# The second layer norm of half 1 applied feature-major, with its moments spread by DMA

## The chip, the cores and the metric

One core of one Trainium2 chip runs the whole program. The metric is the device time of one execution in microseconds. Engines: PE (TensorE), DVE (VectorE), ACT (ScalarE), POOL (GpSimd) and SP (SyncE, which here only issues DMAs). Each works off its own list of instructions in order, and they meet at semaphores.

## The reference, cut to what matters

1024 tokens with 256 features. The first layer is a feed-forward whose weights for a token are one of four 256x256 context matrices, chosen by the token's id; the second is a mixture of 16 experts of width 96, four for each token, and a shared expert. Each layer gets the layer norm of x:

```
_layernorm(x) = (x - mean(x)) / sqrt(var(x) + 1e-5)        # over the 256 features
x = x + xattn(_layernorm(x), ids, ctx, ctx, ctx)
x = x + ffn(_layernorm(x), router, gate_up, down, shared)
  # ffn: scores = sigmoid(x @ router.T); top 4 by scores + bias, their scores divided by their sum
  #      routed = sum_e c_e * (silu(x @ gate_e.T) * (x @ up_e.T)) @ down_e.T, plus the shared expert
```

## The kernel before, in words

The tokens are two halves of 512 (h = 0, 1). All large products are feature-major: features on the partitions, tokens along the row, 512 wide. Every fp32 operand is split into a high part (rounded to fp32r) and a low part, and a product is three matmuls: high by low, high by high, low by high. The high part is made by ACT (or by DVE in the first layer), the low part by DVE (POOL for the weights).

The second layer is a list of 26 items (h, c), where c = 0 is the shared expert with the router's rows, and c = 1 to 12 are chunks of 128 of the 1536 routed features. Its order is (0,0) to (0,8), (1,0), (0,9) to (0,12), (1,1) to (1,12); g is an item's place in it, so place[1, 0] is 9 and place[1, 1] is 14. Pass g on PE (L1078 to L1093) is gate(g), up(g) (six matmuls each) and the down of item g - 2 (six, L1056 to L1059). Pass 11 has no down, and pass 16 has two, for item (1,0) and then for item 14. For each g, ACT makes silu of the gate (`silu_gate`, L528) and the high part of hid (`hid_high`, L538), and DVE the product with the router's weights (`product`, L800), hid (`hidden_2`, L813) and its low part (`hid_low`, L818). PE's gate(g) waits for silu(g - 2), up(g) for hid(g - 2), and down(g - 2) for both parts of hid.

The normalised x of half 1 is wanted at pass 9, and is made during the passes before:
- pass 2, PE: `x1_transposes` turn x1 (feature-major in xt) token-major into banks 5 and 4.
- pass 3, ACT: `copy_x1` moves them into x. DVE: `tile_stats`, `layer_norm_vars` of norm 3, from x. POOL: `rstd_of(3)`, the power -0.5 (L429).
- pass 5, DVE and ACT: `layer_norm_apply(3)`, `apply_norm(3)` write xn, token-major.
- pass 7, PE: `norm_transposes` (L917) turn xn back, eight transposes of 128x128 into banks 4 and 5, between up(7) and the down of item 5.
- pass 8, ACT: `x_high` (L463), DVE: `x_low` (L641), from those banks to xn_hi and xn_lo.

The router's rows of half 1 come out of gate(9). ACT copies them (`router_logits`, L519); DVE transposes them in lanes (`lane_logits`, L704), and over passes 10 to 12 finds the best four and the weights (`lane_best`, `lane_marks`, `lane_rows`). SP writes these to DRAM (`write_rows(1)`) and spreads them over partitions for item 14 on (`spread_rows`). At pass 15 DVE adds half 0's sums to xt (`output(0)`, L825), which frees the two sum banks for the down of item (1,0) at pass 16.

SP's list (L393 to L403) holds, after `write_rows(0)`, for each g the spread of item g (L390), the last two weight loads at g = 4 and 6 (L357), and the outputs. A spread's slot (two in x, two in ids) is free when the product four chunks back is done. POOL's list (L426 to L449) holds the powers and the low parts of the weights in the order of the pieces (`low_part`, L423, two instructions of 128x512 each), the power of norm 3 standing between pieces 10 and 11. ACT makes the high parts of pieces 12, 13 and 14 in passes 5, 6 and 7.

Of the kernel before, what the change touches and what calls it, by code (L numbers as in the profile page):

```python
# [28 lines left out]
P = 128  # L29
TOKENS = 1024  # L30
D = 256
# [19 lines left out]
WARM_UP = 20  # L51
LAG = 2
SENTINEL = -3.0e38
MARK = 3.0e38
# [24 lines left out]
def build(nc, x_d, xt_d, ids_d, ctx_d, bias_d, gu_d, wd0_d, wd_d, consts_d, out_d):  # L79
# [4 lines left out]
    with ExitStack() as ctx:  # L84
# [26 lines left out]
        power = sb("power", [P, TT])  # L111
        xn = sb("xn", [P, TT, D])
        xn_hi = sb("xn_hi", [P, HALVES, KC, HALF], F32R)
        xn_lo = sb("xn_lo", [P, HALVES, KC, HALF], F32R)
# [44 lines left out]
        rows_out, rows_copied = [sem(f"rows_out{h}") for h in range(HALVES)], sem("rows_copied")  # L159
        combt_zero, pick_rows_set, x1_copied = sem("combt_zero"), sem("pick_rows_set"), sem("x1_copied")  # L160
        dstep = sem("dstep")
        varied, powered, shifted = sem("varied"), sem("powered"), sem("shifted")
        normed_v, normed_a = sem("normed_v"), sem("normed_a")
        x1_turned = sem("x1_turned")
        side_done = sem("side_done")
        xhi_done, xlo_done = sem("xhi_done"), sem("xlo_done")
# [19 lines left out]
        for g in range(1, N):  # L186
            if g == 1:
                side_order += [("combt", 0, 0, 4)]
            if g <= BY_MATMUL:
                side_order += [("spread", *items[g], 4 + g % 2)]  # L190
            if g == BY_MATMUL:
                side_order += [("x1", 1, 0, 5), ("x1", 1, 1, 4)]
            if g == place[1, 0] - 2:
                side_order += [("n2", 1, 0, 4), ("n2", 1, 1, 5)]
        side_at = {u[:3]: n for n, u in enumerate(side_order)}

        def wait_side_read(eng, b, n):

            before = [u for u in side_order[:n] if u[3] == b]
            if not before:  # L200
                return
            what, h, k, _ = before[-1]
            if what in ("n1", "n2"):
                count = (HALVES * KC if what == "n2" else 0) + h * KC + k + 1
                eng.wait_ge(xhi_done, count)
                eng.wait_ge(xlo_done, count)
            elif what == "x1":
                eng.wait_ge(x1_copied, k + 1)
            elif what == "spread":
                eng.wait_ge(prod_done, routed(place[h, k]))  # L210
            elif what == "router":
                eng.wait_ge(logit_summed, h + 1)
            else:
                eng.wait_ge(rows_copied, h + 1)
# [119 lines left out]
        def tile_to_norm(n, t):  # L334

            if n != HALVES:
                return x[:, n % HALVES * TT + t]
            at = t % (TT // KC) * D
            return ring_bank("x1", 0, t // (TT // KC))[:, at:at + D]

# [9 lines left out]
        def _(sp):  # L350
# [32 lines left out]
            def spread_rows(g):  # L383
# [5 lines left out]
                for first, last, e in parts_of_chunk(c):  # L389
                    sp.dma_start(spread(n)[first:last],  # L390
                                 comb_d[h, e].partition_broadcast(last - first)).then_inc(spread_in[n % SPREADS], 16)

            write_rows(0)  # L393
            for g in range(BY_MATMUL + 1, N):
                if g == place[1, 1]:
                    write_rows(1)
                if items[g][1] > 0:
                    spread_rows(g)
                if g in (4, 6):
                    load_piece(len(pieces) - 2 + (g == 6))  # L400
                if g == place[1, SPREADS]:
                    write_output(0)
# [4 lines left out]
        def _(pool):  # L407
# [24 lines left out]
            nc.gpsimd.memset(biased_l[:, :, E2:], SENTINEL).then_inc(logits_zero, 1)  # L432
            nc.gpsimd.memset(comb_l[:], 0.0).then_inc(logits_zero, 1)
            nc.gpsimd.memset(combt[:].bitcast(F32), 0.0).then_inc(combt_zero, 1)
            rstd_of(0, 1, slice(0, TT // 2))
# [10 lines left out]
            low_part(early_pieces + 1)  # L446
            rstd_of(3, 5)
            for n in range(early_pieces + 2, len(pieces)):
                low_part(n)  # L449

        @block.scalar
        def _(act):
# [50 lines left out]

            def copy_x1(h):

                act.wait_ge(normed_v, HALVES * TT // 2)
                for pair in range(KC):
                    act.wait_ge(side_done, side_at["x1", h, pair] + 1)
                    at = h * TT + pair * (TT // KC)
                    nc.scalar.activation(x[:, at:at + TT // KC].rearrange("p t d -> p (t d)"),  # L510
                                         side_bank("x1", h, pair)[:], ACT.Copy).then_inc(x1_copied, 1)

# [64 lines left out]
            for g in range(1, N):  # L577
                if g == place[1, 0] - 1:
                    x_high("n2", 1, 0)
                    x_high("n2", 1, 1)  # L580
                if g == place[1, 0] + 1:
                    score(1)
                if g == place[1, 0]:
                    router_logits(1)
                if g == BY_MATMUL + 1:
                    copy_x1(1)
                silu_gate(g)
                if g == 1:
                    combine_rows(0)
                if g in late_pieces:  # L590
                    high_part(late_pieces[g])
                hid_high(g)
                if g == 5:
                    apply_norm(3)

        @block.vector
        def _(dve):
# [8 lines left out]
            def tile_stats(n, t):  # L606
                if n > HALVES:
                    dve.wait_ge(x1_copied, t // (TT // KC) + 1)
                elif n == HALVES:
                    dve.wait_ge(x1_turned, t // (TT // KC) + 1)  # L610
                step(nc.vector.bn_stats(stats[:, t], tile_to_norm(n, t)))  # L611
# [25 lines left out]
            def x_low(what, h, k):  # L637
                n = (HALVES * KC if what == "n2" else 0) + h * KC + k
                dve.wait_ge(xhi_done, n + 1)
                dve.wait_ge(side_done, side_at[what, h, k] + 1)  # L640
                nc.vector.tensor_tensor(xn_lo[:, h, k], side_bank(what, h, k)[:], xn_hi[:, h, k].bitcast(F32),  # L641
                                        ALU.subtract).then_inc(xlo_done, 1)

# [233 lines left out]
            for g in range(1, N):  # L877
                if g == place[1, 0] - 1:
                    x_low("n2", 1, 0)
                    x_low("n2", 1, 1)  # L880
                product(g)
                hidden_2(g)
                if g == place[1, 0]:
                    lane_logits()
# [9 lines left out]
                if g == 3:  # L894
                    for t in range(TT):
                        tile_stats(3, t)
                    layer_norm_vars(3)
                if g == 5:
                    layer_norm_apply(3)
            output(1)  # L900

        @block.tensor
        def _(pe):
# [18 lines left out]
            def x1_transposes(h, pair):  # L922
# [7 lines left out]
                for t in range(TT // KC):  # L930
                    at = h * HALF + (pair * (TT // KC) + t) * P
                    for k in range(KC):
                        ins = nc.tensor.transpose(b[:, t * D + k * P:t * D + (k + 1) * P], xt[:, k, at:at + P],  # L933
                                                  consts_sb[:, 0:P])
                ins.then_inc(x1_turned if h == 0 else side_done, 1)

            def mix(n, between={}):
# [140 lines left out]
            for g in range(1, N):  # L1078
# [4 lines left out]
                if g <= BY_MATMUL:  # L1083
                    spread_weights(g)
                if g == place[1, 0] - 2:
                    norm_transposes("n2", 3, 1)

                if g >= LAG and downs_at[g - LAG]:
                    for n in downs_at[g - LAG]:
                        down(n)  # L1090
                if g == BY_MATMUL:
                    x1_transposes(1, 0)
# [48 lines left out]
```

## Time and profile before

| what | us |
|---|---|
| median of three runs (lowest, highest) | 175.72 (175.63, 175.94) |
| the profiled execution | 175.69 |
| its span, first to last instruction | 173.6 |
| PE busy | 168.2 (97%) |
| DVE, ACT, POOL busy | 117.6, 68.1, 40.3 |

Times in views are from the start of the span. A matmul's row in the timeline overlaps the next one (0.40 long, one each 0.23); the chain of waits gives each the 0.23 that it holds the path for, and there a step stands some 0.16 later than its row in the timeline. An instruction's duration in the timeline counts from where it was issued on its engine, so that it holds time in which it was kept from its operands. The granted clock of PE is 0.999 over the span.

### The profile page before, as it was taken

To read this page: it belongs to the slowest core of one execution; us is meant where nothing else is said; L and a number is where in the kernel's file an instruction comes from. 1 tells how busy PE (TensorE), PEld (TensorE's weight loads), DVE (VectorE), ACT (ScalarE), POOL (GpSimd) and SP (SyncE) were. 2 spreads that over 40 slices of the span, in tenths; PEclk is the share of its full clock that TensorE was granted. 3 is DMA by queue.
4 is the path that set the end of the run, shared out by engine and by line. 5 is a ranking of instruction groups with operands and counts; after the bars stand their busy time and mean duration, and the time that the engine had idled before them with its cause. 6 is when DMAs were issued, how large, how long until landed. Compare 5 with 4: busy or idle time off the path is not lost.

```text
span 173.6 us, 2253 instructions
## 1 busy us (share of the span) xinstructions
PE 168.2 (97%) x738; PEld 131.9 (76%) x738; DVE 117.6 (68%) x267; ACT 68.1 (39%) x108; POOL 40.3 (23%) x41
## 2 busy tenths in 40 slices
PE   6989999999999999999999999999999999999992
PEld 2558888888888878888888788888878888878881
DVE  0779897885588697787688649995874544444452
ACT  2462431343115965724654582222332222222320
POOL 5593011674220006439385000000000000000000
PEclk9999999999999999999999999999999999999999
DMA  4999004065400006951111100004454221100003
GB/s 139 283 414 337 11 0 123 0 178 184 121 0 4 0 4 144 265 144 62 60 60 60 60 0 4 0 0 125 125 194 140 81 66 65 66 5 0 0 0 121
DMA packets 7451, 15.82 MB, mean 91 GB/s; under 512 B 1296, under 2 KB 1904, under 8 KB 7312
## 3 DMA queue, kind: packets, MB, share of 16 engines
q1 hardware_dynamic: 7440, 15.68, 28.5%
q8 instruction: 6, 0.10, 0.2%
q14 instruction: 5, 0.04, 0.1%
HBM read 14.56 MB, written 1.11 MB: 90 GB/s over the span
## 4 chain that ended last, share of the span: by engine, by line
PE 89%; DVE 3%; ACT 3%; DMA 2%; issue 1%; DVEq 0%; ACTq 0%
PE bank L955 24%; PE bank L1038 13%; PE bank L1037 13%; PE bank L1036 13%; PE bank L1056 7%; PE bank L1059 7%; PE bank L1057 7%; DMA x<-x_d 2%; PE bank L917 2%; PE bank L933 1%; DVE stats L611 1%; PE bank L1033 1%; PE bank L1032 1%; ACT L490 1%; ACT xn L480 1%
## 5 line engine op out<-in xcount | busy, mean ns | idle before, releaser
L1038 PE MATMUL bank<-xn_lo,gu_hi 128*128 128x512 f32 (+1 forms) x104 | 41.1, 395 | 0.0
L1036 PE MATMUL bank<-xn_hi,gu_lo 128*128 128x512 f32 x96 | 38.1, 397 | 0.0
L1037 PE MATMUL bank<-xn_hi,gu_hi 128*128 128x512 f32 x96 | 38.0, 395 | 0.0
L538 ACT ACTIVATE h_hi<-hid 128x512 fp32r<-128x512 f32 (+1 forms) x26 | 16.4, 632 | 44.4 <-DVE hid L813 44.4
L818 DVE TENSOR_TENSOR h_lo<-hid,h_hi 128x512 fp32r<-128x512 f32 (+1 forms) x26 | 21.6, 830 | 14.1 <-ACT h_hi L538 14.0
L1038 PEld LDWEIGHTS bank<-xn_lo,gu_hi 128*128 128x128 f32 (+1 forms) x104 | 19.4, 187 | 4.9
L528 ACT ACTIVATE act_sb<-bank 128x512 f32<-128x512 f32 (+1 forms) x26 | 15.4, 592 | 16.7 <-PE bank L1038 16.6
L423 POOL TENSOR_TENSOR gu_lo<-stage,gu_hi 128x512 fp32r<-128x512 f32 x12 | 16.8, 1417 | 21.4 <-ACT gu_hi L456 21.3
L1037 PEld LDWEIGHTS bank<-xn_hi,gu_hi 128*128 128x128 f32 x96 | 18.0, 188 | 4.3
L1036 PEld LDWEIGHTS bank<-xn_hi,gu_lo 128*128 128x128 f32 x96 | 18.0, 188 | 4.2
L662 DVE COPY_PREDICATED prod<-beyond,bank 128x512 f32<-128x512 uint8 x24 | 17.8, 740 | 4.9 <-PE bank L955 3.8
L1056 PE MATMUL bank<-h_hi,wd_lo 128*128 128x512 f32 (+1 forms) x52 | 20.8, 399 | 0.0
L1059 PE MATMUL bank<-h_lo,wd_hi 128*128 128x512 f32 (+1 forms) x52 | 20.6, 395 | 0.0
L1057 PE MATMUL bank<-h_hi,wd_hi 128*128 128x512 f32 (+1 forms) x52 | 20.6, 395 | 0.0
L813 DVE TENSOR_TENSOR hid<-prod,bank 128x512 f32<-128x512 f32 x24 | 16.5, 687 | 1.7
L800 DVE TENSOR_TENSOR prod<-act_sb,ids 128x512 f32<-128x512 f32 x10 | 7.6, 764 | 10.2 <-ACT act_sb L528 8.9
L800 DVE TENSOR_TENSOR prod<-act_sb,x 128x512 f32<-128x512 f32 x12 | 9.3, 778 | 7.1 <-ACT act_sb L528 7.1
L955 PE MATMUL bank<-xn_hi,ctx_hi 128*128 128x512 f32 x32 | 12.8, 400 | 0.7 <-ACT xn_hi L463 0.7
L955 PE MATMUL bank<-h_hi,ctx_hi 128*128 128x512 f32 x32 | 12.9, 403 | 0.0
L955 PE MATMUL bank<-xn_lo,ctx_hi 128*128 128x512 f32 x32 | 12.8, 399 | 0.0
L955 PE MATMUL bank<-xn_hi,ctx_lo 128*128 128x512 f32 x32 | 12.7, 396 | 0.0
L955 PE MATMUL bank<-h_lo,ctx_hi 128*128 128x512 f32 x32 | 12.7, 395 | 0.0
(104 smaller groups left out, 224.1 us busy)
## 6 DMA issues: line engine op xcount, KB each, us to landing
stage<-gu_d SPq DMA_DIRECT2D x6, 512.0 KB, 3.5
stage<-wd_d SPq DMA_DIRECT2D x3, 512.0 KB, 5.1
x<-comb_d SPq DMA_DIRECT2D x8, 192.0 KB, 2.8
ids<-comb_d SPq DMA_DIRECT2D x7, 192.0 KB, 2.7
stage<-ctx_d SPq DMA_DIRECT2D x4, 256.0 KB, 5.3
xt<-xt_d SPq DMA_DIRECT2D x1, 1024.0 KB, 9.5
x<-comb_d SPq DMA_DIRECT2D x8, 128.0 KB, 2.8
ids<-comb_d SPq DMA_DIRECT2D x6, 128.0 KB, 3.3
```

The source lines that it names most:

```text
L423: ins = nc.gpsimd.tensor_tensor(lo[:, s], st[:, s], hi[:, s].bitcast(F32), ALU.subtract)
L662: nc.vector.copy_predicated(prod[:, n % 2], beyond[:, e - 1, h * HALF:(h + 1) * HALF], ring_bank("z", n, e)[:]).then_inc(z_picked, 1)
L800: nc.vector.tensor_tensor(prod[:, g % 2], act_sb[:, g % 2], rows, ALU.mult).then_inc(prod_done, 1)
L813: nc.vector.tensor_tensor(hid[0:w, g % 2], src, up_bank(g)[0:w, :], ALU.mult).then_inc(hid_done, 1)
L818: nc.vector.tensor_tensor(h_lo[0:w, slot[g]], hid[0:w, g % 2], h_hi[0:w, slot[g]].bitcast(F32), ALU.subtract).then_inc(hlo_done, 1)
L955: return nc.tensor.matmul(ring_bank("z", n, e)[:], (ctx_hi, ctx_lo)[a][:, e, k, f], parts[k][b], start=start, stop=stop)
L1036: nc.tensor.matmul(out[:], gu_lo[:, cols], xn_hi[:, h, k], start=(k == 0), stop=False)
L1037: nc.tensor.matmul(out[:], gu_hi[:, cols], xn_hi[:, h, k], start=False, stop=False)
L1038: ins = nc.tensor.matmul(out[0:rows, :], gu_hi[:, wide], xn_lo[:, h, k], start=False, stop=(k == KC - 1))
L1056: nc.tensor.matmul(acc[k][:], wd_lo[0:w, c, cols], hi, start=(c == 0), stop=False)
L1057: nc.tensor.matmul(acc[k][:], wd_hi[0:w, c, cols], hi, start=False, stop=False)
L1059: ins = nc.tensor.matmul(acc[k][:], wd_hi[0:w, c, cols], lo, start=False, stop=(c == ITEMS - 1))
```

## The change

- PE: the eight transposes L917 of pass 7 are gone. In their place, behind down(2) in pass 4, one 128x128 transpose turns a tile `moments` whose columns 0 to 3 are the means of the four token tiles and columns 4 to 7 the rstds, so that rows 0 to 7 of bank 4 are mean and rstd of all 512 tokens.
- DVE: statistics of norm 3 read x1's banks themselves; the means are copied to `moments`; `layer_norm_apply(3)` is gone. In pass 7, between hid and its low part, two multiplications by the rstd row (`x1_scale`); in pass 8 `x1_low` in place of `x_low`, from SBUF.
- ACT: `copy_x1` and `apply_norm(3)` are gone; `copy_moments` (8x128) stands in pass 4 ahead of `hid_high(4)`; `x1_high` in place of `x_high`, from SBUF.
- POOL: one more memset (128x128); the power writes into `moments`; behind low_part(12) two subtractions of the mean row from xt, 128x512 each, ahead of low_part(13).
- SP: behind the spread of item 5, the write of 8x128 to DRAM, a wait for it, and its broadcast to all partitions (512 KB, into xn); all later spreads and the last weight load stand behind.

```diff
+MOMENTS_AT = 4
+CENTRE_BEHIND = 12
+        moments = sb("moments", [P, P])
+        moments_t = sb("moments_t", [2 * TT, P])
+        moments_d = nc.dram_tensor("moments_d", (2 * TT, P), F32, kind="Internal").ap()
+        moments_all = xn[:].rearrange("p t d -> p (t d)")
+        mean_all, rstd_all = moments_all[:, 0:HALF], moments_all[:, HALF:]
+        x1_norm = x[:, TT:].rearrange("p t d -> p (t d)")
...
+            def write_moments():
+                sp.wait_ge(moments_copied, 1)
+                sp.dma_start(moments_d, moments_t[:]).then_inc(moments_out, 16)
+                sp.wait_ge(moments_out, 16)
+                sp.dma_start(moments_all, moments_d.rearrange("r c -> (r c)").partition_broadcast(P)).then_inc(moments_in, 16)
+                if g == MOMENTS_AT + 1:
+                    write_moments()
...
+            nc.gpsimd.memset(moments[:], 0.0).then_inc(moments_zero, 1)
-            rstd_of(3, 5)
+            pool.wait_ge(varied, NORMS + 1)
+            pool.wait_ge(moments_zero, 1)
+            nc.gpsimd.tensor_tensor(moments[:, TT:2 * TT], vareps[:, 3], power[:], ALU.pow).then_inc(powered, 1)
             for n in range(early_pieces + 2, len(pieces)):
                 low_part(n)
+                if n == CENTRE_BEHIND:
+                    for k in range(KC):
+                        pool.wait_ge(moments_in, 16)
+                        nc.gpsimd.tensor_tensor(x1_norm[:, k * HALF:(k + 1) * HALF], xt[:, k, HALF:], mean_all,
+                                                ALU.subtract).then_inc(centred, 1)
...
-            def copy_x1(h):
+            def copy_moments():
+                act.wait_ge(side_done, side_at["moments", 1, 0] + 1)
+                nc.scalar.activation(moments_t[:], side_bank("moments", 1, 0)[0:2 * TT, 0:P], ACT.Copy).then_inc(moments_copied, 1)
+            def x1_high(k):
+                act.wait_ge(x1_normed, k + 1)
+                act.wait_ge(z_done, (mixed[1, 1, KC - 1] + 1) * E1)
+                nc.scalar.activation(xn_hi[:, 1, k], x1_norm[:, k * HALF:(k + 1) * HALF], ACT.Copy).then_inc(xhi_done, 1)
                 if g == place[1, 0] - 1:
-                    x_high("n2", 1, 0)
-                    x_high("n2", 1, 1)
+                    x1_high(0)
+                    x1_high(1)
-                if g == BY_MATMUL + 1:
-                    copy_x1(1)
                 silu_gate(g)
...
+                if g == MOMENTS_AT:
+                    copy_moments()
                 hid_high(g)
-                if g == 5:
-                    apply_norm(3)
...
+            def x1_scale():
+                dve.wait_ge(moments_in, 16)
+                for k in range(KC):
+                    dve.wait_ge(centred, k + 1)
+                    o = x1_norm[:, k * HALF:(k + 1) * HALF]
+                    nc.vector.tensor_tensor(o, o, rstd_all, ALU.mult).then_inc(x1_normed, 1)
+            def x1_low(k):
+                dve.wait_ge(xhi_done, (HALVES + 1) * KC + k + 1)
+                dve.wait_ge(x1_normed, k + 1)
+                nc.vector.tensor_tensor(xn_lo[:, 1, k], x1_norm[:, k * HALF:(k + 1) * HALF], xn_hi[:, 1, k].bitcast(F32),
                                         ALU.subtract).then_inc(xlo_done, 1)
             for g in range(1, N):
                 if g == place[1, 0] - 1:
-                    x_low("n2", 1, 0)
-                    x_low("n2", 1, 1)
+                    x1_low(0)
+                    x1_low(1)
                 product(g)
                 hidden_2(g)
+                if g == place[1, 0] - 2:
+                    x1_scale()
...
                     layer_norm_vars(3)
-                if g == 5:
-                    layer_norm_apply(3)
+                    dve.wait_ge(moments_zero, 1)
+                    nc.vector.tensor_copy(moments[:, 0:TT], meanvar[:, 3, :, 0]).then_inc(means_set, 1)
...
+            def moments_transpose():
+                pe.wait_ge(means_set, 1)
+                pe.wait_ge(powered, NORMS + 1)
+                b = side_wait("moments", 1, 0)
+                nc.tensor.transpose(b[:, 0:P], moments[:], consts_sb[:, 0:P]).then_inc(side_done, 1)
...
-                if g == place[1, 0] - 2:
-                    norm_transposes("n2", 3, 1)
                 if g >= LAG and downs_at[g - LAG]:
                     for n in downs_at[g - LAG]:
                         down(n)
+                if g == MOMENTS_AT:
+                    moments_transpose()
```

## Rows read from the trace of the kernel before

**Rows 1.** The page: busy time by engine, and the chain's share by engine.

```profile
PE 168.2 (97%) x738; PEld 131.9 (76%) x738; DVE 117.6 (68%) x267; ACT 68.1 (39%) x108; POOL 40.3 (23%) x41
...
PE 89%; DVE 3%; ACT 3%; DMA 2%; issue 1%; DVEq 0%; ACTq 0%
```

**Rows 2.** The chain in order of time, passes 5 to 9: start, length, what.

```profile
78.20 0.23 PE bank L1036
...
86.60 0.23 PE bank L1036
...
89.40 0.87 PE bank L917 x8
...
91.66 0.23 PE bank L1036
...
95.86 0.23 PE bank L1032
```

**Rows 3.** The same, pass 16: the first matmul of item (1,0)'s down.

```profile
126.65 0.50 PE bank L1056
```

**Rows 4.** Who waited for whom: us in total, times, longest.

```profile
PEld bank L1056 <- DVE xt L825: 0.4, 1, 0.4
```

**Rows 5.** Timeline of DVE: start, length, line, what, idle before.

```profile
99.45 0.71 DVE L704 STREAM_TRANSPOSE comb_row<-logits 32x512 f32<-32x512 f32 x1
...
121.27 0.69 DVE L800 TENSOR_TENSOR prod<-act_sb,ids 128x512 f32<-128x512 f32 x1 [1.31 <-DMA ids<-comb_d]
```

**Rows 6.** Timeline of POOL and DVE about the powers of norms 2 and 3.

```profile
50.25 1.01 POOL L429 TENSOR_TENSOR rstd<-vareps,power 128x4 f32<-128x4 f32 x1 [5.66 <-DVE vareps L620]
...
76.62 0.69 DVE L800 TENSOR_TENSOR prod<-act_sb,x 128x512 f32<-128x512 f32 x1
...
76.79 1.39 POOL L429 TENSOR_TENSOR rstd<-vareps,power 128x4 f32<-128x4 f32 x1 [5.30 <-DVE vareps L620]
```

**Rows 7.** Timeline of all engines about the combine transposes.

```profile
61.71 0.40 PE L1038 MATMUL bank<-xn_lo,gu_hi 128*128 128x512 f32 x1
...
61.98 0.22 DVE L782 TENSOR_TENSOR comb_parts<-comb_parts 128x64 fp32r<-128x64 f32 x1
...
62.64 0.47 PE L1036 MATMUL bank<-xn_hi,gu_lo 128*128 128x512 f32 x1
```

**Rows 8.** Timeline of ACT, passes 4 and 9.

```profile
78.06 0.64 ACT L538 ACTIVATE h_hi<-hid 128x512 fp32r<-128x512 f32 x1 [2.03 <-DVE hid L813]
...
97.34 0.59 ACT L519 ACTIVATE logits<-bank 32x512 f32<-32x512 f32 x1 [0.28 <-PE bank L1038]
```

**Rows 9.** DMA issues, whole span, then 71 to 78: KB each, us to landing.

```profile
stage<-gu_d SPq DMA_DIRECT2D x6, 512.0 KB, 3.5
...
comb_d<-comb_row SPq DMA_DIRECT2D x2, 32.0 KB, 1.6
...
stage<-gu_d SPq DMA_DIRECT2D x1, 512.0 KB, 5.8
```

**Rows 10.** Timeline of POOL, passes 5 to 7, in narrow windows.

```profile
82.81 1.29 POOL L423 TENSOR_TENSOR gu_lo<-stage,gu_hi 128x512 fp32r<-128x512 f32 x1
...
87.37 2.99 POOL L423 TENSOR_TENSOR wd_lo<-stage,wd_hi 128x512 fp32r<-128x512 f32 x2 [3.26 <-ACT wd_hi L456]
...
88.62 1.74 POOL L423 TENSOR_TENSOR wd_lo<-stage,wd_hi 128x512 fp32r<-128x512 f32 x1
```

**Rows 11.** Timeline of DVE, passes 7 and 8.

```profile
88.48 0.73 DVE L818 TENSOR_TENSOR h_lo<-hid,h_hi 128x512 fp32r<-128x512 f32 x1 [0.70 <-ACT h_hi L538]
89.14 1.77 DVE L800 TENSOR_TENSOR prod<-act_sb,x 128x512 f32<-128x512 f32 x1
90.94 0.69 DVE L813 TENSOR_TENSOR hid<-prod,bank 128x512 f32<-128x512 f32 x1
...
93.80 1.27 DVE L641 TENSOR_TENSOR xn_lo<-bank,xn_hi 128x512 fp32r<-128x512 f32 x2
...
95.71 0.69 DVE L813 TENSOR_TENSOR hid<-prod,bank 128x512 f32<-128x512 f32 x1
```

More of the change, by code:

```diff
@@ L159, in build @@
         rows_out, rows_copied = [sem(f"rows_out{h}") for h in range(HALVES)], sem("rows_copied")
-        combt_zero, pick_rows_set, x1_copied = sem("combt_zero"), sem("pick_rows_set"), sem("x1_copied")
+        combt_zero, pick_rows_set = sem("combt_zero"), sem("pick_rows_set")
         dstep = sem("dstep")
@@ L164, in build @@
         x1_turned = sem("x1_turned")
+        moments_zero, means_set, moments_copied = sem("moments_zero"), sem("means_set"), sem("moments_copied")
+        moments_out, moments_in = sem("moments_out"), sem("moments_in")
+        centred, x1_normed = sem("centred"), sem("x1_normed")
         side_done = sem("side_done")
@@ L192, in build @@
                 side_order += [("x1", 1, 0, 5), ("x1", 1, 1, 4)]
-            if g == place[1, 0] - 2:
-                side_order += [("n2", 1, 0, 4), ("n2", 1, 1, 5)]
+            if g == MOMENTS_AT:
+                side_order += [("moments", 1, 0, 4)]
         side_at = {u[:3]: n for n, u in enumerate(side_order)}
@@ L207, in wait_side_read @@
             elif what == "x1":
-                eng.wait_ge(x1_copied, k + 1)
+                eng.wait_ge(varied, NORMS + 1)
+            elif what == "moments":
+                eng.wait_ge(moments_copied, 1)
             elif what == "spread":
@@ L334, in tile_to_norm @@
         def tile_to_norm(n, t):
[L336 to L339, printed above, removed]
+            at, pair = t % (TT // KC) * D, t // (TT // KC)
+            if n < HALVES:
+                return x[:, n * TT + t]
+            if n == HALVES:
+                return ring_bank("x1", 0, pair)[:, at:at + D]
+            return side_bank("x1", 1, pair)[:, at:at + D]
         def wait_normed(eng, n, t):
@@ L502, in combine_rows @@
                 nc.scalar.activation(comb_row[2 * E2:3 * E2, h], side_bank("combt", h, 0)[2 * E2:3 * E2, :], ACT.Copy).then_inc(rows_copied, 1)
-            def copy_x1(h):
[L506 to L511, printed above, removed]
+            def copy_moments():
[5 more added lines that the diff above has]
+                nc.scalar.activation(xn_hi[:, 1, k], x1_norm[:, k * HALF:(k + 1) * HALF], ACT.Copy).then_inc(xhi_done, 1)
             def router_logits(h):
@@ L607, in tile_stats @@
                 if n > HALVES:
-                    dve.wait_ge(x1_copied, t // (TT // KC) + 1)
+                    dve.wait_ge(side_done, side_at["x1", 1, t // (TT // KC)] + 1)
                 elif n == HALVES:
@@ L641, in x_low @@
                 nc.vector.tensor_tensor(xn_lo[:, h, k], side_bank(what, h, k)[:], xn_hi[:, h, k].bitcast(F32),
+                                        ALU.subtract).then_inc(xlo_done, 1)
+            def x1_scale():
[8 more added lines that the diff above has]
+                nc.vector.tensor_tensor(xn_lo[:, 1, k], x1_norm[:, k * HALF:(k + 1) * HALF], xn_hi[:, 1, k].bitcast(F32),
                                         ALU.subtract).then_inc(xlo_done, 1)
@@ L1084, in _ @@
                     spread_weights(g)
-                if g == place[1, 0] - 2:
-                    norm_transposes("n2", 3, 1)
                 if g >= LAG and downs_at[g - LAG]:
@@ L1090, in _ @@
                         down(n)
+                if g == MOMENTS_AT:
+                    moments_transpose()
                 if g == BY_MATMUL:
```

## Prediction, made before the result was known

> **What bounds the kernel now.** I read the busy shares and the shares of the chain first: PE is busy 97% of the span and has 89% of the chain [rows 1]. Then the chain in order of time: the passes of the second layer (g = 1 to 25, one per item) stand on a fixed grid. A pass is 12 matmuls of gate and up and 6 of down, 4.20 us (91.66 to 95.86); pass 7 holds the eight L917 transposes besides and takes 5.06 (86.60 to 91.66), so they cost **0.86 us of PE's path**, not hidden by anything [rows 2]. Last, the waits and the late part of the chain: PE waits once for another engine in this stretch, at 126.65, for DVE's output of half 0 before the down of item (1,0): that step is 0.50 instead of 0.23, so 0.27 lost [rows 3, 4]. That output stands at the end of a chain of DVE and ACT work that begins at pass 9 (router logits, lane transpose at 99.45, best four, rows to DRAM, spread back with a DMA wait at 121.27) [rows 5]. So two things end together: PE's grid, and this router chain, which is already 0.27 late.
>
> **Part 1, the transposes go.** -0.86 us on PE at pass 7, if nothing else is late [rows 2].
>
> **Part 2, the moments' transpose at pass 4.** PE comes to it after down(2), at 78.20 on the chain, its weight load being wanted one matmul and some (0.39) earlier, at 77.81. It waits for the power on POOL. The statistics now read PSUM instead of x, and the ACT copies go; but DVE is held before them by h_lo(3), so their place stays. Before, POOL's power starts at 76.79 and ends at 78.18; it takes 1.39 against 1.01 at 50.25, as prod (L800, two SBUF inputs) ran from 76.62 to 77.31 [rows 6]. The new copy of the means (four columns) shifts that product by 0.08, so the power ends at 78.26: 0.45 late. What such lateness costs is seen at the combine transposes: their input lands at 62.20 (61.98 + 0.22), 0.49 after the load of L1038's successor was due (61.71), and the next gate matmul comes 0.93 after L1038, where four transposes at 0.11 and one step of 0.23 make 0.67: 0.26 to 0.3 lost [rows 7]. So 0.28 for the wait and 0.11 for the transpose itself (0.86/8): **+0.39**. Bounds: 0.11 if the power gets in ahead of the product (then it ends at 77.8), 0.8 if it is held by a whole further op. Passes 5 to 7 run 0.39 late, pass 8 on 0.47 early; pass 9 would start at 95.39.
>
> **Part 3, ACT and SP at pass 4.** copy_moments stands ahead of hid_high(4), which ran at 78.06 [rows 8]; the copy can start near 78.75 and takes about 0.3 (an estimate: ACT's smallest rows are 0.26 to 0.6), so hid_high(4) ends at 79.6. down(4) wants it at pass 6: hidden. SP then writes the 4 KB (1.6 to land, as comb_d) and issues the 512 KB broadcast at 80.65. It lands in 3.5 us as the free weight loads do, or 5.8 as the load at 71.56 that shared the queue with spreads: 84.2 to 86.4 [rows 9]. I take 84.8, as the queue is empty when it is issued. Behind the two waits on SP stand the spreads of items 6, 7 and 8 and the last weight load, about 1.3 MB, which before were under way by then; at the pace of [rows 9] they land from 85 to 89.5, about when DVE and ACT want them. The new memset on POOL ends before POOL's first power and costs nothing.
>
> **Part 4, POOL and DVE, the deciding part.** x_low read a PSUM bank (L641, two in 1.27) [rows 11]. Now there are two subtractions on POOL of the form of its low parts, 1.29 each when free, and on DVE two multiplications and two x1_low whose inputs both lie in SBUF. The rows show that such a DVE op and a POOL op exclude each other: prod at 89.14 took 1.77 instead of 0.69, ending 0.55 after POOL's pair that began at 87.37 (so its own 0.69 began 0.14 before POOL's end); and POOL's second op took 1.74 instead of 1.29 as h_lo held it at 88.48. hid at 90.94, with a PSUM input, ran its 0.69 under a busy POOL. And they alternate: h_lo and prod stood back to back on DVE, and POOL got in between them [rows 10, 11].
>
> The Trainium skill, SBUF — State Buffer, "Who interferes with whom", says that a DVE instruction with two SBUF inputs contends with a GpSimd instruction that reads SBUF, one with at most one SBUF input does not, and whoever issues first holds the shared pair for the whole instruction; the trace agrees (1.77 against 0.69). It does not say who is next when both want it; if DVE kept it over two ops in a row, the sum would be that of rival A.
>
> Queued behind the new waits are, on POOL, low_part(13) and (14) behind centre, and on DVE h_lo(7) and pass 8 behind the two scales. By 0.69, 1.29 and 0.14 at each handover, in us: POOL ends low_part(12) at 84.4 (82.81 + 1.29 and 0.26 for the later silu and h_lo(4)) [rows 10]; centre(0) 84.8 to 86.1; prod(6) is held to 86.0-86.6; centre(1) 86.5-87.8; hid(6) 86.7-87.4, ACT's h_hi(6) to 88.0; low_part(13) has POOL 87.8-89.1 and 89.5-90.8 with h_lo(6) between them (to 89.6); prod(7) 90.6-91.3; hid(7) to 92.0; low_part(14) first half 91.2-92.5; scale(0) 92.3-93.0; second half 92.9-94.2; scale(1) 94.05-94.7. DVE then is free of POOL: h_lo(7) to 95.4, x1_low(0) to 96.0, x1_low(1) to 96.7, prod(8), hid(8) to **98.07**. Before, hid(8) ended at 96.40 (95.71 + 0.69) [rows 11]. With the broadcast at 85.0 and prod(6) first, the order differs but h_lo(7) waits for the last POOL op and hid(8) again ends at 98.07.
>
> **Part 5, what this does.** PE at pass 9 wants x1_low(0) at 95.39 + 0.47 - 0.39 = 95.47 and has it at 96.0: some 0.45 lost. That alone would make the change worth nothing (-0.86 + 0.39 + 0.45). But ACT does h_hi(8) after hid(8), then the router's logits, then silu(9), and DVE hid(9) and the lane transpose. In order these take 0.03 + 0.6 + 0.6 + 0.6 + 0.03 + 0.72 = 2.58, so the lane transpose starts at 98.07 + 2.58 = 100.65 instead of 99.45: **1.2 us later**; before it was PE's gate(9) that set it (logits at 97.34 waited 0.28 for PE) [rows 5, 8]. From there to the output at pass 15 every piece is DVE, ACT or DMA in a row, with no POOL work left and no slack (the chain ends 0.27 after PE asks). So PE, wherever it stands meanwhile (on the old grid within 0.1), waits about 1.4 at down of item (1,0), and all that follows is 1.2 later than before.
>
> **Sum.** The profiled execution took 175.69, of which 173.6 is the span; the median of the three runs is 175.72, 0.03 more. Span 173.6 + 1.2 = 174.8, time 175.72 + 1.2 = **176.9**.
>
> **Rivals.**
> A, faster: DVE keeps the port over ops back to back, or is never held long. Then h_lo(6), prod(7) end by 90.3, the two scales by 92.7, x1_low(1) by 94.6, hid(8) by 96.0. That is before the point that decides, hid(8) at 96.4: there PE's gate(9) sets the logits, and the whole chain moves with PE. 175.72 - 0.86 + 0.39 = 175.25. For it: POOL's spans are rough, and one pair of rows is all there is on who comes next. Against it: the alternation at 89.14 [rows 10, 11].
> B, much slower: the broadcast or the spreads land late, 5.8 us instead of 4.1 [rows 9]. centre(0) runs 86.4-87.7, each later POOL op falls between two DVE ops, x1_low(0) itself is held to 96.8, and hid(8) ends at 98.84: 96.87 is the value at which the lane chain is unmoved, so +1.97, 177.7. For it: 1.3 MB queue up behind the moments.
> C, no change: the router chain has slack that I don't see, and only the waits of pass 4 and pass 9 count: -0.86 + 0.39 + 0.45 = 0, 175.7. Against it: PE's wait at 126.65 [rows 3, 4].
>
> **Chances.** Forecast 0.52, A 0.16, B 0.20, C 0.12. 0.2% (0.35 us) is about what a measurement of this kernel tells from no change. A is faster; C is mostly the same (0.09), else slower (0.03); with the forecast and B that is 0.75 slower. The range is 175.4 to 178.0: it takes in B, C and the bound of 0.8 of part 2, and leaves out the middle of A and a pile-up worse than B. The forecast's own range is 176.2 to 177.3, hid(8) at 97.4 to 98.5.
>
> **What would show it.** L917 has 24 transposes instead of 32, and pass 7 is 4.2 us. Pass 4 to 5 shows 0.4 us more on PE, with the power named as releaser. The multiplications by rstd, or h_lo(7) and prod(7), last over 1.2 us while POOL works. hid of item 8 ends near 98; the lane transpose (L704's line) starts near 100.6; PE's step at down of item (1,0) is near 1.6 instead of 0.50. If hid(8) ends before 96.4 and that step is still 0.5, A is right; if the lane transpose is late but PE's step at pass 16 is not long, C is.

## The result, and the profile after

The changed kernel takes 177.38 us (median of 6) against 175.75: ratio 1.0089, interval 1.007 to 1.0107, **slower by 1.6 us**. The forecast was 176.9 in 175.4 to 178.0. One of the six, the profiled one, ran at a granted clock of 0.66 and took 239.26 us; the ratio is without it, and the median of the other five is 177.15. The profile shown is therefore that of a repeat run of the same kernel, `after_same`: median 176.99, ratio 1.0083, profiled execution 177.43, the longest of its four.

The page's heads, which answer to [rows 1]: PE's share falls from 97% to 95%, and of the chain that ended last from 89% to 61%; DVE and DMA now have 25% of it.

```profile
span 175.6 us, 2241 instructions
...
PE 167.3 (95%) x731; PEld 130.7 (74%) x731; DVE 118.3 (67%) x267; ACT 66.8 (38%) x105; POOL 42.5 (24%) x44
...
PE 61%; DVE 15%; DMA 10%; ACT 6%; issue 5%; SPq 1%; DVEq 0%; ACTq 0%
```

PE's timeline, in the three places where it now stands still (start, length, line): pass 4, pass 9, and the down of item (1,0) at pass 16.

```profile
77.37 0.40 PE L1114 MATMUL bank<-h_lo,wd_hi 128*128 128x512 f32 x1
77.92 0.30 PE L990 MATMUL bank<-consts_sb,moments 128*128 128x128 f32 x1 [0.16 <-issue]
78.05 0.47 PE L1091 MATMUL bank<-xn_hi,gu_lo 128*128 128x512 f32 x1
78.36 0.39 PE L1092 MATMUL bank<-xn_hi,gu_hi 128*128 128x512 f32 x1
...
95.15 0.40 PE L1088 MATMUL bank<-xn_hi,gu_lo 128*96 128x512 f32 x1
96.44 0.50 PE L1093 MATMUL bank<-xn_lo,gu_hi 128*128 128x512 f32 x1 [0.89 <-DVE xn_lo L687]
96.77 0.39 PE L1087 MATMUL bank<-xn_hi,gu_hi 128*128 128x512 f32 x1
...
126.62 0.40 PE L1093 MATMUL bank<-xn_lo,gu_hi 128*128 128x512 f32 x1
128.31 0.50 PE L1111 MATMUL bank<-h_hi,wd_lo 96*128 96x512 f32 x1 [1.29 <-DVE xt L871]
```

The step at pass 16 in PE's timeline of the kernel before, which answers to [rows 3]:

```profile
126.24 0.40 PE L1038 MATMUL bank<-xn_lo,gu_hi 128*128 128x512 f32 x1
126.65 0.50 PE L1056 MATMUL bank<-h_hi,wd_lo 96*128 96x512 f32 x1
```

A matmul follows the last by 0.23 where nothing holds it. So pass 4 costs 0.45 more (77.37 to 78.05 is 0.68, less 0.23), pass 9 1.06 more (1.29 less 0.23), and the step at pass 16 is 1.69 from start to start, where it was 0.41 before: 1.28 more. The matmul behind each new wait also starts late, after 0.31 and 0.33 instead of 0.23. With -0.86 for the transposes these make 0.45 + 0.08 + 1.06 + 0.10 + 1.28 - 0.86 = +2.11.

Executions differ ahead of the second layer and behind the last matmul: here the front is 0.45 shorter after the change and the tail 0.33 longer. So I compare profiles by T, the time from the start of PE's first x1 transpose of half 1 (68.78 before, 68.33 after) to the start of its last matmul (169.91, 171.58): 101.13 before, **103.25** after, +2.12, which these terms account for.

What DVE and POOL do in passes 6 to 9, the answer to [rows 11] and [rows 10]:

```profile
87.01 1.64 DVE L846 TENSOR_TENSOR prod<-act_sb,ids 128x512 f32<-128x512 f32 x1 [2.56 <-DMA ids<-comb_d]
88.69 0.69 DVE L859 TENSOR_TENSOR hid<-prod,bank 128x512 f32<-128x512 f32 x1
90.08 0.69 DVE L864 TENSOR_TENSOR h_lo<-hid,h_hi 128x512 fp32r<-128x512 f32 x1 [0.70 <-ACT h_hi L571]
91.08 0.69 DVE L846 TENSOR_TENSOR prod<-act_sb,x 128x512 f32<-128x512 f32 x1 [0.31 <-DMA x<-comb_d]
91.80 0.69 DVE L859 TENSOR_TENSOR hid<-prod,bank 128x512 f32<-128x512 f32 x1
92.41 2.77 DVE L681 TENSOR_TENSOR x<-x,xn 128x512 f32<-128x512 f32 x2
95.10 0.68 DVE L864 TENSOR_TENSOR h_lo<-hid,h_hi 128x512 fp32r<-128x512 f32 x1
95.70 1.28 DVE L687 TENSOR_TENSOR xn_lo<-x,xn_hi 128x512 fp32r<-128x512 f32 x2
96.90 0.68 DVE L846 TENSOR_TENSOR prod<-act_sb,x 128x512 f32<-128x512 f32 x1
97.62 0.69 DVE L859 TENSOR_TENSOR hid<-prod,bank 128x512 f32<-128x512 f32 x1
...
100.96 0.71 DVE L750 STREAM_TRANSPOSE comb_row<-logits 32x512 f32<-32x512 f32 x1
```

```profile
84.16 2.71 POOL L479 TENSOR_TENSOR x<-xt,xn 128x512 f32<-128x512 f32 x2 [0.26 <-DMA xn<-moments_d]
86.82 2.99 POOL L446 TENSOR_TENSOR wd_lo<-stage,wd_hi 128x512 fp32r<-128x512 f32 x2
91.56 3.07 POOL L446 TENSOR_TENSOR gu_lo<-stage,gu_hi 128x512 fp32r<-128x512 f32 x2 [1.75 <-ACT gu_hi L487]
```

hid of item 8 ends at 98.31 (96.40 before), the two scales take 2.77 under POOL's low parts, and the lane transpose starts at 100.96 (99.45 before [rows 5]). But there is a wait that the forecast had as hidden: prod(6) stands 2.56 us for its spread. The DMA view of 76 to 90 us (busy tenths of the DMA engines in 40 slices of 0.35 us; then issues, KB each, median us to landing) shows why. The spread of item 6 is issued behind the broadcast and ahead of the last weight load, the spreads of items 7 and 8 behind both, and the engines are nearly full from 81 to 89.

```profile
DMA  0000000000000069999599884999999999999745
...
ids<-comb_d SPq DMA_DIRECT2D x3, 192.0 KB, 6.1
xn<-moments_d SPq DMA_DIRECT2D x1, 512.0 KB, 4.3
stage<-gu_d SPq DMA_DIRECT2D x1, 512.0 KB, 8.3
...
x<-comb_d SPq DMA_DIRECT2D x1, 192.0 KB, 6.1
x<-comb_d SPq DMA_DIRECT2D x1, 64.0 KB, 8.7
```

### The profile page after: what moved, and what is told of

The parts are those of the page before. It is cut to its first block, busy times and chain, and to the rows that moved or that the text cites. A ratio compares the mean times of both kernels' runs of the same rounds, so it can differ in the third digit from the quotient of the medians.

```text
span 237.4 us, 2241 instructions
## 1 busy us (share of the span) xinstructions
PE 231.9 (98%) x731; PEld 146.2 (62%) x731; DVE 115.6 (49%) x267; ACT 68.2 (29%) x105; POOL 41.0 (17%) x44
## 4 chain that ended last, share of the span: by engine, by line
PE 98%; ACT 0%; POOL 0%; DVE 0%; issue 0%; DVEq 0%; POOLq 0%
PE bank L1010 26%; PE bank L1093 14%; PE bank L1091 13%; PE bank L1092 13%; PE bank L1112 7%; PE bank L1111 7%; PE bank L1114 7%; PE bank L1123 3%; PE bank L965 2%; PE bank L1088 1%; PE bank L981 1%; PE bank L1087 1%; PE bank L1038 0%; PE bank L1045 0%; ACT xn_hi L494 0%; PE bank L1055 0%
## 5 line engine op out<-in xcount | busy, mean ns | idle before, releaser
L1093 PE MATMUL bank<-xn_lo,gu_hi 128*128 128x512 f32 (+1 forms) x104 | 52.9, 509 | 0.0
L1091 PE MATMUL bank<-xn_hi,gu_lo 128*128 128x512 f32 x96 | 49.1, 512 | 0.0
L1092 PE MATMUL bank<-xn_hi,gu_hi 128*128 128x512 f32 x96 | 48.7, 507 | 0.0
L1112 PE MATMUL bank<-h_hi,wd_hi 128*128 128x512 f32 (+1 forms) x52 | 26.5, 510 | 0.0
L1111 PE MATMUL bank<-h_hi,wd_lo 128*128 128x512 f32 (+1 forms) x52 | 26.3, 507 | 0.0
L1114 PE MATMUL bank<-h_lo,wd_hi 128*128 128x512 f32 (+1 forms) x52 | 26.2, 504 | 0.0
L1010 PE MATMUL bank<-xn_hi,ctx_hi 128*128 128x512 f32 x32 | 16.4, 511 | 0.6 <-ACT xn_hi L494 0.6
L1010 PE MATMUL bank<-h_hi,ctx_hi 128*128 128x512 f32 x32 | 16.5, 516 | 0.0
L1010 PE MATMUL bank<-xn_lo,ctx_hi 128*128 128x512 f32 x32 | 16.3, 508 | 0.0
L1010 PE MATMUL bank<-h_lo,ctx_hi 128*128 128x512 f32 x32 | 16.3, 508 | 0.0
```

What stands on the lines that cost most here:

```text
L1010: return nc.tensor.matmul(ring_bank("z", n, e)[:], (ctx_hi, ctx_lo)[a][:, e, k, f], parts[k][b], start=start, stop=stop)
L1091: nc.tensor.matmul(out[:], gu_lo[:, cols], xn_hi[:, h, k], start=(k == 0), stop=False)
L1092: nc.tensor.matmul(out[:], gu_hi[:, cols], xn_hi[:, h, k], start=False, stop=False)
L1093: ins = nc.tensor.matmul(out[0:rows, :], gu_hi[:, wide], xn_lo[:, h, k], start=False, stop=(k == KC - 1))
L1111: nc.tensor.matmul(acc[k][:], wd_lo[0:w, c, cols], hi, start=(c == 0), stop=False)
L1112: nc.tensor.matmul(acc[k][:], wd_hi[0:w, c, cols], hi, start=False, stop=False)
```

## Experiments

The question after the result: is the loss the port between POOL and DVE (the forecast), the spreads that come late behind the moments (rival B), or PE's own waits (rival C); and is the router chain really without slack? Times stand against runs of the kernel before on the same chip.

**1. after_same**: the changed kernel unchanged.

> The changed kernel as it is, for a profile at full clock. My theory (the recorded forecast, with the measured 1.009): span 175.2 to 175.8. hid of item 8 ends at 98.0 to 98.7, the lane transpose starts near 100.6 to 101.2, and PE's step at the down of item (1,0), pass 16, is 1.6 to 2.1 us instead of 0.50. Rival (only PE's own waits at passes 4, 9 and between): the time is lost on PE before pass 10, and the step at pass 16 stays near 0.5.

Measured: as shown above. The long step at pass 16 is there (1.69), and so is a loss at pass 9 (1.06) that was larger than forecast. The rival, loss before pass 10 alone, is out.

**2. hold_pool**: POOL's last low parts wait.

```diff
             for n in range(early_pieces + 2, len(pieces)):
+                if n == CENTRE_BEHIND + 1:
+                    pool.wait_ge(xlo_done, NORMS * KC)
                 low_part(n)
```

> The changed kernel with POOL's low parts of the last two weight pieces held until both x1_low are done, so that they no longer meet the scales and x1_low on DVE. Port theory: the scales and h_lo(7) run in 0.69 each, hid of item 8 ends by 96.5, PE loses nothing at pass 9, the whole is 0.8 to 1.6 us faster than the changed kernel (175.6 to 176.5; the low parts now meet product(8) and h_lo(8) instead). Rival (the moments arrive late by DMA, the port is not it): within 0.3 of the changed kernel, 177.2.

Measured: 175.97, ratio 1.0019 (1.0004 to 1.0035), 1.1 us better than the changed kernel. The scales run at 0.69 each and PE loses nothing at pass 9:

```profile
87.16 0.69 DVE L848 TENSOR_TENSOR prod<-act_sb,ids 128x512 f32<-128x512 f32 x1 [2.54 <-DMA ids<-comb_d]
...
92.14 1.28 DVE L683 TENSOR_TENSOR x<-x,xn 128x512 f32<-128x512 f32 x2
93.34 0.69 DVE L866 TENSOR_TENSOR h_lo<-hid,h_hi 128x512 fp32r<-128x512 f32 x1
...
95.87 0.69 DVE L861 TENSOR_TENSOR hid<-prod,bank 128x512 f32<-128x512 f32 x1
97.26 1.53 DVE L866 TENSOR_TENSOR h_lo<-hid,h_hi 128x512 fp32r<-128x512 f32 x1 [0.70 <-ACT h_hi L573]
...
100.16 1.32 DVE L755 TENSOR_TENSOR laned<-comb_row 32x256 f32<-32x256 f32 x1
```

The port is the larger cause: 1.1 us is won with the low parts only moved. The late spread stays (2.54), and the held low parts now meet h_lo(8) and laned (1.32 instead of 0.42), on the router chain: the step at pass 16 is still 1.48.

**3. low_memset**: the two last low parts as memsets.

```diff
+                if n > CENTRE_BEHIND:
+                    pool.wait_ge(w_hi, n + 1)
+                    for part in range(2):
+                        s = slice(part * STAGE // 2, (part + 1) * STAGE // 2)
+                        ins = nc.gpsimd.memset(piece_aps(n)[3][:, s].bitcast(F32), 0.0)
+                    ins.then_inc(w_lo, 1)
+                    continue
                 low_part(n)
```

> Leaves out work: the low parts of the last two weight pieces are set to zero by POOL memsets, which read nothing from SBUF, instead of being computed. Port theory: nothing is left on POOL that reads SBUF after the two subtractions of the mean; hid of item 8 ends at 95.5 to 96.3, the lane transpose starts at or before 99.4, and the time is 175.2 to 175.6 (before less 0.86 plus 0.4). Rival (late moments or spreads): 177.0 to 177.4, as the changed kernel.

Measured: 175.52, ratio 0.9996 (0.9973 to 1.0019): 1.5 us better than the changed kernel, as the port theory has it. The single executions lie from 175.2 to 176.8, and the profiled one was the slowest: there the moments' write took 2.35 us instead of 1.19, prod(6) stood 3.96 for its spread, hid(8) ended at 97.87 and the lane transpose started at 100.52. So the expected hid(8) and lane transpose were missed in that profile while the median met the time. With no low part left to meet DVE, what is late there comes by DMA: that path is a cause of its own, and a varying one.

**4. late_lanes**: before, with 1.3 us of DVE work ahead of the lane transpose.

```diff
                 if g == place[1, 0]:
+                    for part in range(KC):
+                        src = ctx_hi[:, part].rearrange("p k f -> p (k f)").bitcast(F32)
+                        dve.wait_ge(w_hi, E1)
+                        dve.wait_ge(w_lo, E1)
+                        dve.wait_ge(z_done, len(mixes) * E1)
+                        nc.vector.tensor_tensor(ctx_lo[:, part].rearrange("p k f -> p (k f)"), src, src, ALU.add)
                     lane_logits()
```

> The kernel before, with two DVE additions of 128x512 whose result nobody reads put ahead of the lane transpose in pass 9 (1.3 us). If the router chain has no slack, as I hold, PE's step at pass 16 grows from 0.50 to 1.8 and the time from 175.7 to 177.0. If it has slack (rival C), the time stays at 175.7 to 175.9.

Measured: 176.14, ratio 1.002 (1.0001 to 1.0039), neither: 0.35 of the 1.3 comes through in the ratio, 0.58 in T of the one profile. The timelines of DVE and ACT show slack at one place in the chain, first in the kernel before, then in this run:

```profile
100.19 0.42 DVE L707 TENSOR_TENSOR laned<-comb_row 32x256 f32<-32x256 f32 x1
...
100.10 1.28 ACT L490 ACT_TABLE_LOAD   x1
```

```profile
100.97 0.42 DVE L707 TENSOR_TENSOR laned<-comb_row 32x256 f32<-32x256 f32 x1
...
99.04 0.64 ACT L538 ACTIVATE h_hi<-hid 96x512 fp32r<-96x512 f32 x1 [0.89 <-DVE hid L813]
99.69 1.28 ACT L490 ACT_TABLE_LOAD   x1
101.42 0.41 ACT L493 ACTIVATE scores_l<-laned 32x256 f32<-32x256 f32 x1 [0.45 <-DVE laned L707]
```

The sigmoid needs laned and the table load; before, laned is ready at 100.61 and the load is through at 101.38, so that laned has 0.8 of slack. Here laned is ready at 101.39 and the load through at 100.97, and the sigmoid waits 0.45 for laned. So in the kernel before the chain does not run over the lane transpose but over silu(9), hid(9), h_hi(9) and the table load on ACT.

**5. late_act**: before, with 1.15 us of ACT work in that path.

```diff
                     router_logits(1)
+                    act.wait_ge(w_lo, E1)
+                    act.wait_ge(z_done, len(mixes) * E1)
+                    for part in range(KC):
+                        nc.scalar.activation(ctx_lo[:, part], ctx_hi[:, part].bitcast(F32), ACT.Copy)
```

> The kernel before, with two ACT copies of 128x512 whose result nobody reads put between the router's logits and silu(9) in pass 9 (1.2 us). late_lanes showed 0.8 us of slack between laned and the sigmoid, as the load of the sigmoid table behind h_hi(9) was later than laned. If the chain runs through ACT (silu(9), hid(9), h_hi(9), table load) and has no slack there, product(10) starts 1.1 to 1.2 later and PE's step at pass 16 grows from 0.4 to 1.5, time 176.8 to 177.0. If the chain has slack there too, the time stays under 176.2.

Measured: 176.88, ratio 1.0061 (1.0039 to 1.0083): +1.07 for 1.15 put in, 0.7 to 1.5 by the interval. PE's step at pass 16 is 1.68 (0.41 before). With that, what the forecast needed of the chain is shown: ACT's lateness in pass 9 is PE's at pass 16, about one to one.

**6. spreads_first**: the changed kernel, moments behind the spreads on SP.

```diff
-                if g == MOMENTS_AT + 1:
+                if g == MOMENTS_AT + 4:
                     write_moments()
```

> The changed kernel with the moments' write and broadcast issued on SP behind the spreads of items 6, 7 and 8 and the last weight load, which then no longer wait for the moments (in the changed kernel prod(6) and prod(7) waited 2.56 and 0.31 for those spreads). DMA theory (the late spreads are the cause of about 1 us of the loss, the port of the rest): hid of item 8 ends 0.7 to 1.7 us earlier than 98.3, PE's loss at pass 9 falls from 1.06 to 0.5 or less, and the time is 175.8 to 176.6. Rival (the port alone sets it, as my working before had it): hid of item 8 still ends at 98.0 or later, 176.9 to 177.2.

Measured: 177.25, ratio 1.0081 (1.0059 to 1.0104): no gain (T of the one profile is 102.81, 0.44 below the changed kernel). The time is the rival's: no product of passes 6 to 8 waits for a spread any more, and now the port takes all of it. The edit is not a clean removal of the DMA's part, though. The moments are now the ones that come late: the broadcast is issued at 81.43 instead of 79.76, and POOL's subtractions start at 85.70 instead of 84.16, having waited 1.41 for it, which puts its low parts later too.

```profile
87.17 1.63 DVE L864 TENSOR_TENSOR h_lo<-hid,h_hi 128x512 fp32r<-128x512 f32 x1 [0.70 <-ACT h_hi L571]
89.16 1.35 DVE L846 TENSOR_TENSOR prod<-act_sb,x 128x512 f32<-128x512 f32 x1 [0.36 <-ACT act_sb L561]
...
91.14 2.77 DVE L681 TENSOR_TENSOR x<-x,xn 128x512 f32<-128x512 f32 x2
93.84 1.78 DVE L864 TENSOR_TENSOR h_lo<-hid,h_hi 128x512 fp32r<-128x512 f32 x1
...
97.46 0.69 DVE L859 TENSOR_TENSOR hid<-prod,bank 128x512 f32<-128x512 f32 x1
```

This is the forecast's own order of events: h_lo(6), prod(7), the scales and h_lo(7) each held by a POOL instruction. hid(8) ends at 98.15, where the forecast had 98.07, and the front is that of before (first x1 transpose at 68.74 against 68.78). PE's loss at pass 9 is 0.49 (a step of 0.72, less 0.23), where the forecast had 0.45, and the step at pass 16 is 1.81.

**7. spreads_hold**: edits 2 and 6 together.

> The same, and POOL's low parts of the last two pieces held until both x1_low are done. If late spreads and the port together explain the loss, hid of item 8 ends by 95.8 and the time is 175.3 to 175.9, at or below the kernel before. If something else makes the chain late (the moments' own path over DRAM), it is no better than hold_pool, 176.0.

Measured: 175.69, ratio 0.9996 (0.998 to 1.0012). hid(8) ends at 94.73 and T is 100.90. Both causes gone, the change costs nothing, and gains nothing yet.

**8. moments_ready**: PE turns other data in pass 4, which leaves out the right moments.

```diff
-                pe.wait_ge(means_set, 1)
-                pe.wait_ge(powered, NORMS + 1)
                 b = side_wait("moments", 1, 0)
-                nc.tensor.transpose(b[:, 0:P], moments[:], consts_sb[:, 0:P]).then_inc(side_done, 1)
+                nc.tensor.transpose(b[:, 0:P], xt[:, 0, HALF:HALF + P], consts_sb[:, 0:P]).then_inc(side_done, 1)
```

> The changed kernel, whose PE turns 128 columns of xt instead of the moments in pass 4, so that it waits for nothing there (leaves out the right moments: the norm of half 1 is wrong). The wait of PE (0.45 with the transpose itself) shrinks to 0.11. My theory: PE's grid is not what ends last at pass 16, so the gain is not 0.34; what counts is that the moments leave for DRAM 0.35 earlier, and with them the spreads: the time falls by 0.2 to 0.4, to 176.6 to 177.0, with the step at pass 16 as long as before or longer. Rival (PE's grid counts): the step at pass 16 stays the same and everything is 0.34 earlier. If the spreads' lateness comes from the amount of data and not from when it starts: no change at all, 177.1.

Measured: 176.64, ratio 1.0058 (1.0038 to 1.0078), some 0.4 better than the changed kernel by the ratios (1.0083 and 1.0089), though the intervals overlap. That is what my theory and the first rival both give, and the step at pass 16, 1.45, came out shorter than either had. prod(6) waits 0.73 for its spread instead of 2.56. But `after_out` (experiment 12), which is the changed kernel with PE's wait left in and differs from it only from pass 15 on, has the same in its profile: prod(6) waits 0.88 and hid(8) ends at 97.57, here at 97.55.

```profile
85.53 0.83 DVE L846 TENSOR_TENSOR prod<-act_sb,ids 128x512 f32<-128x512 f32 x1 [0.88 <-DMA ids<-comb_d]
...
96.88 0.69 DVE L859 TENSOR_TENSOR hid<-prod,bank 128x512 f32<-128x512 f32 x1
```

So the spread's wait in the changed kernel varies from execution to execution, and this experiment does not decide what sets it.

**9. moments_mid**: spreads_hold, with the moments turned where PE need not wait.

```diff
                 gate_or_up(g, False)
+                if g == MOMENTS_AT + 1:
+                    moments_transpose()
...
-                if g == MOMENTS_AT:
-                    moments_transpose()
...
+                hid_high(g)
                 if g == MOMENTS_AT:
                     copy_moments()
-                hid_high(g)
```

> spreads_hold, with the moments' transpose between gate(5) and up(5), 1.4 us later, so that PE doesn't wait for the power, and the copy behind h_hi(4) on ACT. PE's 0.45 at pass 4 becomes 0.11, gate(9) and with it the router chain come 0.34 earlier; the moments land about 1.1 later, which the scales (DVE gets to them near 90) don't feel. My theory: 0.3 us faster than spreads_hold, 175.3 to 175.5, ratio 0.997 to 0.9985. Rival: the router chain takes its own time from its DMAs on and nothing is gained, 175.7.

Measured: 175.07, ratio 0.9953 (0.9937 to 0.997), faster than before by 0.8 us, and by the ratios 0.8 below spreads_hold (taken on another chip), where 0.3 was expected. T is 100.77, 0.36 below before and 0.13 below spreads_hold (100.90); where the rest of the 0.8 comes from, the profile of one execution does not show. The step at pass 16 is 0.77 here and 0.54 in spreads_hold: the router chain ends last again.

**10. moments_mid_out**, **11. before_out**, **12. after_out**: output(0) ahead of product(15), on moments_mid, on before and on the changed kernel.

```diff
+                if g == place[1, 1] + 1:
+                    output(0)
                 product(g)
                 hidden_2(g)
...
-                if g == place[1, 1] + 1:
-                    output(0)
                 hid_low(g)
```

> moments_mid, with output(0) on DVE ahead of product(15) instead of behind hid(15), so that the router chain ends 1.3 us earlier as PE sees it. If that chain was what ended last at pass 16, PE's step there falls to 0.23 and the time to 175.0 to 175.3, ratio 0.9955 to 0.998. If hid(15), now later, holds up(17), no gain against moments_mid.

> The kernel before with output(0) ahead of product(15). PE's step at pass 16, 0.50 with 0.18 to 0.27 of wait, becomes 0.23: 175.4 to 175.6, ratio 0.9985 to 0.9995.

> The changed kernel with output(0) ahead of product(15). If its loss is the router chain at pass 16 (1.3 us) and PE's wait at pass 9 (1.06) is hidden behind it, the step at pass 16 falls from 1.6 to 0.25 to 0.5, and the time by 1.1 to 1.4, to 175.6 to 175.9: what is left is -0.86 + 0.45 + 1.06 - 0.2 = +0.45 against before. Rival (PE's own waits are the whole loss): the same as the changed kernel, 177.1.

Measured: 174.90, ratio 0.9934 (0.9911 to 0.9956); 175.38, ratio 0.9971 (0.9955 to 0.9986); 176.00, ratio 1.0007 (0.9984 to 1.0029). In all three PE's step at pass 16 is 0.23. The first two are faster than expected (0.9955 to 0.998, and 0.9985 to 0.9995), the third slower (175.6 to 175.9).

The one order on DVE gives the changed kernel 1.3 to 1.4 us (1.0083 or 1.0089 to 1.0007) and the kernel before 0.5. Like against like, the change costs 1.5 to 1.6 us with output(0) behind hid(15), and 0.6 with it ahead of product(15) (1.0007 against 0.9971, two intervals that just meet). So the rival, PE's own waits as the whole loss, is out: 0.8 to 0.9 us of the loss was the router chain at pass 16. That the 0.6 that is left is PE's waits at passes 4 and 9 is argued and not shown. In the profile of after_out PE hardly waits at pass 9 (a step of 0.32) and T is 100.83, against 100.87 for before_out; but that execution, 175.20, is the second fastest of twelve between 175.05 and 177.19.

The version moments_mid_out has the lowest ratio of all and beats both kernels:

```profile
123.66 1.28 DVE L873 TENSOR_TENSOR xt<-bank,xt 128x512 f32<-128x512 f32 x2
124.85 0.68 DVE L848 TENSOR_TENSOR prod<-act_sb,ids 128x512 f32<-128x512 f32 x1
125.57 0.69 DVE L861 TENSOR_TENSOR hid<-prod,bank 128x512 f32<-128x512 f32 x1
...
125.87 0.40 PE L1095 MATMUL bank<-xn_lo,gu_hi 128*128 128x512 f32 x1
126.10 0.40 PE L1113 MATMUL bank<-h_hi,wd_lo 96*128 96x512 f32 x1
```

Its T is 100.10: 1.03 below before, of which before_out has 0.26 (the old wait at pass 16). The other 0.77 is what the change was worth on PE's path once nothing else was late: about 0.86 less one transpose of 0.11.

## Why the prediction was right, and where not

- **The transposes, -0.86**: right. It shows as a gain only in experiments 9 and 10.
- **PE's wait at pass 4, +0.39**: measured 0.45, and 0.53 with the late matmul behind it. On the clock of before the power ends at 78.27 (76.37 + 1.45, and 0.45 for the shorter front), where the forecast had 78.26. The timeline calls the wait "issue", not the power as the forecast wanted; PE's weight load starts at 77.89, behind the power's end at 77.82.
- **The port (part 4)**: right in kind and in size. Experiment 6 has the forecast's order of events and its hid(8) within 0.1; experiments 2 and 3 take POOL's last low parts out of the way and win 1.1 to 1.5. POOL and DVE alternated at the scales too (two in 2.77, not 1.28), so rival A's premise fell. By the Trainium skill, SBUF — State Buffer, "Who interferes with whom", the order of issue decides which of the two is blocked. The trace agrees as far as it goes: the second scale, issued at 93.40 while POOL's second half ran from 92.89 to 94.63, took 1.78.
- **The landing of the spreads (part 3), forecast as about in time**: this step failed. In the profile after, prod(6) waited 2.56 us and prod(7) 0.31; in other executions with the same SP list prod(6) waited 0.73 to 3.96. Rival B named the spreads but priced the broadcast (4.3 to land, I had 4.1); late were the spreads issued behind it, 4.0 to 8.7 us where before they took 2.8 in the median. The lateness did not add to the port's. While prod(6) stood still, POOL worked off low parts that DVE would have met, and h_lo(6), prod(7) and h_lo(7) then ran free in 0.69, 0.69 and 0.68, so that hid(8) ended at 98.31 all the same. The port's cause taken away alone gives back nearly all or all (1.0019, 0.9996), both together all (0.9996). The DMA's alone was not taken away cleanly (experiment 6, 1.0081), so its share is open.
- **PE's loss at pass 9, +0.45**: mis-sized, 1.06, since x1_low(0) came later: 96.38, which is 96.83 on the clock of before, where the forecast had 96.0. Its own times, 95.47 and 96.0, make 0.53 and not 0.45. While the router chain is the later one, PE's wait at pass 9 comes out of its wait at pass 16, so that the error did not count in the sum.
- **The router chain without slack (part 5)**: right as a whole (experiments 5 and 12), with its path mis-drawn. I ran it over the lane transpose, where there is 0.8 of slack; it runs over h_hi(9) and the table load. Both were late by the same 1.5 (laned ready at 102.12, the load through at 102.89), so the sum did not suffer. From hid(8)'s end to the lane transpose I had 2.58; it is 2.65.
- **The size**: 1.2 forecast, 1.6 measured (1.2 to 1.9 by the interval), and 2.1 in T of the profile shown. The term that was too small there is hid(8)'s end. On the clock of before it is 98.76 in that profile (98.31 and 0.45 for the shorter front), 0.7 later than the forecast's 98.07. In after_out's it is 97.80, and there the lateness is smaller than forecast. So the forecast lies among executions that differ by a microsecond with the landing of the spreads, which it did not foresee; that its sum came within 0.4 of the measured time is in part luck.

## What to carry to other kernels

A step taken off the busiest engine is worth what it takes only if no second chain ends with it; find the place where the two meet (here one wait of 0.27 us at pass 16) and ask who is late there after the change. An instruction that reads PSUM and one that reads two SBUF tiles cost the same on DVE (hid and prod, 0.69 each) until POOL works beside it (prod 1.77, hid still 0.69). A wait put on the DMA-issuing engine delays everything in its list, and here those transfers then landed together, in 4.0 to 8.7 us instead of 2.8.

## What was not expected of the hardware

- The 4 KB write to DRAM took 1.19 us in the profiles of after_same and hold_pool, 2.35 in that of low_memset, whose program is the same up to there. In spreads_first the broadcast behind it was issued 2.48 after it.
- Spreads of 64 to 192 KB, which landed in 2.8 us in the median of before (5.3 at most), took 4.0 to 8.7 when issued in a row behind a 512 KB broadcast, with a 512 KB load among them. In after_out's profile the same row took 3.2 to 5.6.
